# Half-row pairs for keys and values, scores in three PSUM banks, picks two batches late, first pair of row writes behind the first normalise

## The reference, cut to what matters

```python
# attention: 16 heads of 64; the last 4 of the 77 context rows have keys and values of their own
q   = xn @ Wq + lora(xn)
k,v = ctx[:73] @ Wk + lora(ctx), ctx[:73] @ Wv + lora(ctx)
out = attention(q, k, v) + attention(q, ctx[73:] @ Wk_ipa, ctx[73:] @ Wv_ipa)
x1  = x + out @ Wo + bo + lora(out)
# feed-forward: 8 experts, the best 2 of each token
logits = x2n @ gate_w                     # x2n = layernorm(x1)
top_logits, top_idx = top_k(logits, 2);   w = softmax(top_logits)
y   = x1 + sum over the two picks of w * (silu(x2n @ w1[e]) @ w2[e])
```

## Time and profile before

| what | value |
|---|---|
| median of the runs (3: 783.06, 783.86, 788.45) | 783.86 us |
| the profiled execution: its time / its span | 784.63 / 782.8 us |
| granted TensorE clock, mean of the span | 0.967 |
| busy share: PE / DVE / POOL / ACT | 87 / 68 / 63 / 58 % |
| batch bodies 1 to 14, from the first scores of one to those of the next | 27.4 us (27.7 in three of them) |

### The profile page before, as it was taken

The page is one execution under the profiler, slowest core; times in us unless marked ns, Lnnn a source line. Parts: engine busy times, 40 slices in busy tenths (PEclk is TensorE's granted clock), DMA queues, the critical chain, the costliest instruction groups (busy, mean ns, idle before and its releaser), DMA issues.

```text
span 782.8 us, 23092 instructions
## 1 busy us (share of the span) xinstructions
PE 684.6 (87%) x7980; PEld 574.2 (73%) x7981; DVE 534.7 (68%) x1226; ACT 454.8 (58%) x772; POOL 494.8 (63%) x584
## 2 busy tenths in 40 slices
PE   6747799999999999999999998751999999999994
PEld 2225688788787878878787887540888898888993
DVE  5963687877887797788779778633555565555552
ACT  1545878687776867777777777520433434344441
POOL 3125556786788678778868877853265656556565
PEclk9998899999999999999999999885999999999998
DMA  9901001111111111111111111015255555554550
GB/s 250 305 30 43 28 17 50 48 44 52 55 54 42 48 48 41 55 55 54 42 41 54 42 55 55 28 42 188 49 83 87 94 89 92 90 95 76 84 90 1
DMA packets 41676, 54.69 MB, mean 70 GB/s; under 512 B 6320, under 2 KB 36016, under 8 KB 41648
## 3 DMA queue, kind: packets, MB, share of 16 engines
q1 hardware_dynamic: 26176, 35.90, 15.7%
q0 software_dynamic: 14384, 17.33, 12.8%
q10 hardware_dynamic: 1088, 1.08, 0.4%
HBM read 30.36 MB, written 25.76 MB: 72 GB/s over the span
## 4 chain that ended last, share of the span: by engine, by line
PE 48%; DVE 16%; issue 13%; POOL 7%; ACT 6%; DMA 5%; SPq 4%; POOLq 1%; DVEq 0%; ACTq 0%
PE ps L1319 39%; DVE pt_s L1072 4%; DVE sm L1150 3%; PE ps L1380 3%; POOL prob L729 2%; PE ps L1401 2%; DVE picks L1213 2%; ACT x2n L936 2%; PE ps L439 2%; DMA pt_s<-in_wo 2%; POOL rows_dram L785 2%; DMA out_x<-pt_s,token_of 1%; POOL out_x L413 1%; DVE q_s L1072 1%; DVE x_sb L1171 1%
## 5 line engine op out<-in xcount | busy, mean ns | idle before, releaser
L413 POOL DMA_INDIRECT out_x<-pt_s,token_of x78 | 125.4, 1608 | 31.6 <-issue 30.9
L492 ACT ACTIVATE q_s<-ps 128x512 f32<-128x512 f32 x78 | 46.6, 598 | 133.1 <-PE ps L1319 132.4
L565 DVE TENSOR_TENSOR ot_s<-q_s,ot_s 128x512 f16<-128x512 f32 x78 | 54.0, 693 | 85.9 <-ACT ot_s L496 59.5
L1319 PE MATMUL ps<-q_s,ffnw 128*128 128x256 f16 x936 | 109.9, 275 | 0.0
L1319 PE MATMUL ps<-ffnw,ot_s 128*128 x936 | 108.7, 273 | 0.2 <-issue 0.2
L729 POOL TENSOR_TENSOR prob<-prob,mx 128x1168 f32<-128x1168 f32 x64 | 77.7, 1235 | 36.1 <-DVE mx L1143 35.8
L1319 PEld LDWEIGHTS ps<-ffnw,ot_s 128*128 128x128 f16 x936 | 90.2, 98 | 13.4 <-issue 2.0
L1319 PEld LDWEIGHTS ps<-q_s,ffnw 128*128 x936 | 90.6, 99 | 10.9 <-issue 0.5
L1319 PE MATMUL ps<-xt_s,wq_s 128*128 128x256 f16 x768 | 91.9, 282 | 6.4 <-DVE q_s L1072 4.5
L1319 PEld LDWEIGHTS ps<-xt_s,wq_s 128*128 128x128 f16 x768 | 77.4, 101 | 18.3 <-DVE q_s L1072 4.7
L1319 PE MATMUL ps<-wo_s,ot_s 128*128 128x256 f16 x768 | 89.2, 273 | 1.9 <-DVE ot_s L1072 1.9
(11 more groups left out here) (179 smaller groups left out, 1283.8 us busy)
## 6 DMA issues: line engine op xcount, KB each, us to landing
prob<-rows_dram SPq DMA_DIRECT2D x39, 264.0 KB
wstage<-in_ffn_w SPq DMA_DIRECT2D x16, 512.0 KB, 3.5
x_sb<-in_x SPq DMA_DIRECT2D x4, 1024.0 KB, 12.8
out_x<-x_sb SPq DMA_DIRECT2D x16, 256.0 KB, 2.2
out_x<-pt_s,token_of POOLq DMA_INDIRECT x78
rows_dram<-wstage ACTq DMA_DIRECT2D x4, 264.0 KB
rows_dram<-wstage SPq DMA_DIRECT2D x4, 264.0 KB
pt_s<-in_wq SPq DMA_DIRECT2D x2, 512.0 KB, 4.5
```

What stands on the lines that cost most here:

```text
L413: pool.indirect_dma_start(out_rows, bass.IndirectOffsetOnAxis(ap=token_of[:, j % UNROLL, c:c + 1], axis=0), y_sb[:, j % UNROLL, c, :], Non ...
L492: act.activation(h32[:, half, :], h_ps(j, half), ACT.Silu, scale=1 / WSCALE).then_inc(silu_done, 1)
L565: dve.tensor_tensor(hs[:, j % 2, 1, 2 * half:2 * half + 2, :].rearrange("p f n -> p (f n)"), h32[:, half, :], hs[:, j % 2, 0, 2 * half:2 * ...
L1319: last = pe.matmul(o, lhs(a, n), rhs(c, n), start=(i == 0), stop=(i == len(steps) - 1))
```

## The change

The diff makes five edits and rearranges the bodies around them.

1. **Half-row pairs.** The 64 rest rows of the context and of the key and value weights no longer stand above 64 zero rows. The rest rows of even head pairs (for values: of the first 512 columns) lie in partitions 0 to 63, those of odd ones in 64 to 127. A product of the rest has 64 rows, and two of them, one in each half, follow each other into two PSUM banks. The low memory fills with zeros fall away. The context rest of a batch is copied by two small transfers (ctx_k, ctx_v), issued by SP a batch ahead.
2. **Scores in three banks.** The 16 heads' scores lie 5, 5 and 6 to a bank in banks 0 to 2 (before: four in each of banks 0 to 3). A new semaphore, s_thirds, keeps the two row halves from writing one bank at a time. Other results change banks too.
3. **Late picks.** `pick_experts`, `place_rows`, `rank` and `weigh_picks` of batch b-2 run in body b; before, those of b-1 did, at the end of body b. In the last body's wake the routing of batch 14 now stands before that of 15.
4. **Row writes.** The first pair of batch b-2 stands behind `normalise(b, 0)`, the second behind `normalise(b, 1)`; before, they stood before `shift(b, 0)` and before `shift(b, 1)`.
5. **Order on PE and ACT.** Values and keys are each made in one piece; `row_high` stands between the second and third of the head results on ACT; body 1 is written out before the loop.

```diff
-        wk_s = sb("wk_s", [P, 2, KD, ID], F16)
-        wv_s = sb("wv_s", [P, 2, KD, ID], F16)
+        wk_s = sb("wk_s", [P, 2, CW], F16)
+        wv_s = sb("wv_s", [P, 2, CW], F16)
+        ctx_k = sb("ctx_k", [P, 2, ORG], F16)
+        ctx_v = sb("ctx_v", [P, 2, ORG], F16)
...
-            return ps[:, (6, 7, 4, 6)[k], :]
+            return ps[:, (6, 7, 4, 0)[k], :]
...
+        PAIR_BANKS = ((0, 1), (0, 1), (0, 1), (0, 2), (0, 2), (0, 2), (1, 2), (1, 2))
...
-            for kk, rows in enumerate((P, CDR)):
-                sp.dma_start(cstage[kk][0:rows, 0:BATCH * CTX], ctx_t[kk * P:kk * P + rows, :]
-                             ).then_inc(ctx_in[kk], 16)
+            sp.dma_start(cstage[0][:, 0:BATCH * CTX], ctx_t[0:P, :]).then_inc(ctx_in[0], 16)
+            for half in (0, 1):
+                sp.dma_start(cstage[1][half * CDR:half * CDR + CDR, 0:BATCH * CTX], ctx_t[P:CD, :]
+                             ).then_inc(ctx_in[1], 16)
...
             def body(b):
-                first, settled = isinstance(b, int) and b == 0, not (isinstance(b, int) and b < 2)
-                if settled:
-                    scatter(b - 2)
+                first, routed = isinstance(b, int) and b == 0, not (isinstance(b, int) and b < 2)
+                if routed:
+                    router_gap(b - 2)
+                    weigh_picks(b - 2)
                 shift(b, 0)
-                if settled:
-                    scatter_pick(1)
                 shift(b, 1)
                 normalise(b, 0)
+                if routed:
+                    scatter(b - 2, 0)
                 if not first:
                     rstd_2(b - 1)
                 normalise(b, 1)
+                if routed:
+                    scatter(b - 2, 1)
...
                 if not first:
-                    router_gap(b - 1)
                     row_low(b - 1)
-                    weigh_picks(b - 1)
...
                 pt(b, 6)
                 pt(b, 7)
+                ot(b, 0)
+                ot(b, 1)
                 if not first:
                     row_high(b - 1)
-                ot(b, 0)
-                if not first:
-                    gap_e(b - 1)
-                for k in range(1, 4):
-                    ot(b, k)
+                ot(b, 2)
+                ot(b, 3)
...
             def body(b, first, last):
+                routed = not (isinstance(b, int) and b < 2)
+                if routed:
+                    chain = pick_experts(b - 2)
                 maxima(b, 0)
                 if not last:
                     xt(b + 1)
+                if routed:
+                    place_rows(b - 2, chain)
                 maxima(b, 1)
...
+            def key_products(w, m, out, ctx, rest):
+
+                for half in (0, 1):
+                    o = (2 * m + half) * P
+                    for i, (a, c) in enumerate(THREE):
+                        pe.matmul(out[half], w[:, a, o:o + P], ctx(c), start=(i == 0), stop=False)
+                for i, (a, c) in enumerate(THREE):
+                    for half in (0, 1):
+                        last_of[0] = pe.matmul(
+                            out[half], w[half * CDR:half * CDR + CDR, a, ID + m * P:ID + m * P + P], rest(c, half),
+                            start=False, stop=(i == 2))
...
                 for m in range(PAIRS):
+                    if m == 6:
+                        pe.wait_ge(s_thirds, 2 * b + t + 1)
+                    if m == 3:
+                        last.then_inc(s_thirds, 1)
...
                 if not first:
                     project(b - 1, 0)
+                if not (isinstance(b, int) and b < 2):
+                    rank(b - 2)
                 scores(b, 1)
                 if not first:
                     project(b - 1, 1)
...
-                    pe.wait_ge(q_split, 4 * b + 5)
+                pe.wait_ge(s_copied, 2 * b + 2)
+                if not last:
                     queries(b + 1, 3)
-                    pe.wait_ge(q_split, 4 * b + 6)
...
+                if not last:
+                    pe.wait_ge(q_split, 4 * b + 8)
+                    pe.wait_ge(v_split, 2 * b + 1)
+                    new_keys(b + 1)
+                pe.wait_ge(v_split, 2 * b + 2)
                 transpose_probs(b, 4)
```

More of the change, by code:

```diff
@@ L976, in body @@
                 v(b, 0)
+                v(b, 1)
                 if first:
@@ L1369, in scores, with new_values @@
+            def new_values(b):
+                pe.wait_ge(ctx_v_in, 16 * b + 16)
+                value_products(wv_s, [values_bank(half)[0:ORG, :] for half in (0, 1)], lambda part: context(part, b),
+                               lambda part, half: ctx_v[half * CDR:half * CDR + CDR, part, :])
+                last_of[0].then_inc(v_mm, 1)
             def scores(b, t):
@@ L1478, in body @@
             def body(b, first, last):
-                if not first:
-                    pe.wait_ge(slots, b)
                 scores(b, 0)
@@ L1532, in body @@
                     pe.wait_ge(pt_split, 8 * b + 5 + k)
-                    if k in (1, 2) and not last:
-                        pe.wait_ge(k_split, 2 * b + 2 + k)
+                    if k == 1 and not first:
+                        pe.wait_ge(slots, b)
+                        router(b - 1)
                     attend(b, k)
-                    if k == 1 and not first:
-                        rank(b - 1)
             body(0, True, False)
-            with pe.Fori(1, BATCH - 1) as b:
+            body(1, False, False)
+            with pe.Fori(2, BATCH - 1) as b:
                 body(b, False, False)
             body(BATCH - 1, False, True)
-            for t in range(TPB):
-                project(BATCH - 1, t)
+            project(BATCH - 1, 0)
+            rank(BATCH - 2)
+            project(BATCH - 1, 1)
             transpose_2(BATCH - 1)
+            pe.wait_ge(slots, BATCH)
             router(BATCH - 1)
```

344 lines of the change are left out of this document (184 added, 160 removed).

## The result

The changed kernel takes **773.4 us** (median of 4 runs, 771.5 to 774.1), the kernel before 784.0 us in the same session: a ratio of 0.985, 95% interval 0.982 to 0.988. The forecast was 769, the range 753 to 787. The profiled execution took 773.27 us, of which 771.4 is the span.

A forecast was written before the change was run, and what follows sets the result against it. PE bound a body, POOL close behind; after the change POOL's path sets 26.45 us instead of 27.42. Bodies 2 to 15 -13.6, body 1 -2.7, body 0 -2.2, setup +0.1, tail +3.3: -15.1, so 769 us, range 753 to 787.

The forecast's parts named there:

- POOL's path: Shifts, normalises and row writes on POOL: second normalise ends at 20.25 and binds, so a body falls from 27.42 to 26.45 us.
- I take 0, since the neighbouring rows are the same kind of change: Alternating full-row and half-row products among keys and values on PE: a change of array shape costs 0.
- The late signal: ACT's first copy began 0.5 us after the scores' modelled end; taken as 0, +5 to +9 if both scores stall.
- the starts leave nothing between them: Half-row scores beside the full-row output product on PE: no gap seen in the trace, so a shape change costs 0.
- the lost 0.85 us wait: PE's gap of 0.85 us before the ranks, which waited for the picks; forecast to go.
- PE's work falls by 0.9 us: Half-row pairs in a body: keys 1.30 us instead of 1.62, values 1.98 instead of 2.58, PE's work to 24.5.
- The rival of PE's floor: POOL's path is shorter than summed, so PE binds and bodies 2 to 15 take 24.8 us: 746 us, chance 0.09.
- Body 1, body 0, setup: Body 1 without row writes, ranks or weights -2.7 us; body 0 -2.2 us; setup, with context rest rows loaded twice, +0.1.
- Tail: After the last attend, batch 14's row writes delay POOL: rstd_2 of batch 15 at 12.1 instead of 8.8, +3.3 us.
- the rival of the shape change: Shape changes lengthen the keys before the transposes of tile 1, deciding from 0.27 us each: 798 at 0.33, chance 0.09.
- PE is closed there: Sign the forecast is wrong: PE not idle before the first transposes of tile 1, where over 1 us idle was forecast.
- The second pair of writes holds ACT: Slower rival: ACT's row_high waits for the second pair's landing; at 5.0 us landing +17, 801 us, chance 0.05.

The follow-up runs named there:

- keys full: The changed kernel with the keys' last 64 context rows in full-height products against a zero-padded context tile: 764.2 us, ratio 0.974 to the kernel before.
- row_low last: The kernel before with one line moved, POOL's row_low behind the weights of the picks instead of ahead of them: 773.2 us, ratio 0.985.
- the best kernel here: "place in PSUM" with POOL's first pair of row writes between the shifts and the second behind the table's low half: 752.7 us, ratio 0.959.
- place in PSUM: "keys full" with ACT's row_high behind the last head copy and DVE's place written to PSUM instead of SBUF: 757.8 us, ratio 0.967.

## Why the prediction was right, point by point

- *The time.* 773.4 stands 4.4 us above the 769 forecast, inside its own spread of 759 to 779.
- *The bodies, right partly by luck.* 26.60 against 26.45. POOL's path was sized well: output product at 1.79 (forecast 1.75), second shift done at 11.16 (10.95), first normalise at 13.54 (13.4), guard and two writes 2.71 (3.00), `rstd_2` 1.24 (1.36), second normalise at 19.87 (20.25). But it did not bind in the changed kernel. The step that failed is "I take 0, since the neighbouring rows are the same kind of change": a change of shape costs 0.10 us, the eight at the keys 0.8, and the keys start 0.3 later than forecast (17.95). They end at 20.1, where the forecast had them at 18.95 and PE idle until 20.25. Since POOL is done at 19.87, this costs the body only the 0.08 us by which those transposes start earlier in "keys full". The second error weighs more: from the transposes of tile 1 to the end of the body I had 6.1 us, and it takes 6.49, of which 0.26 is the wait for the late signal. POOL's path, 0.38 shorter than forecast, offsets nearly all of that. With the keys repaired POOL binds at 26.19, 0.26 below the forecast.
- *The late signal, seen and put at nothing.* The forecast noted that ACT's first copy began 0.5 us after the scores' modelled end, and looked for the reason in s_thirds or the array's shape. In that trace the scores' signal is 0.49 to 1.24 us late in the 14 bodies that have row writes, where a pair begins 0.09 us before the scores' end; in "row_low last", where the pair begins 1 us behind them, it is on time in all 16. The change took the writes away from the scores and put the second pair beside the transposes of b-1.
- *The rule weighed against the trace.* The Trainium skill (TensorEngine Tiling (Array Packing), Key Properties) says that changing the tiling mode drains the TensorE. The measured 0.10 us agrees in that a change costs something, at half the latency of one key product (0.197 us) and below the 0.16 from which the forecast saw it matter. It does not look like a full drain: the next product starts 0.125 us behind the last one of the other shape, before that one's end as the profile models it. The reading "the starts leave nothing between them" was wrong. In the trace of before, too, the first full product behind the scores starts 0.125 us after the last score product, where starts within one shape are 0.03 to 0.04 apart; the merged rows hide it.
- *The source of the gain, missed in its size.* The forecast counted the lost 0.85 us wait as one of several terms on a new path. "row_low last" gets as much from that wait alone, so that the other parts of the change together come to about zero: bodies 2 to 14 0.09 us shorter (26.60 against 26.68), body 1 1.2 us shorter, setup and body 0 1.2, body 15 and the tail 3.7 longer.
- *Keys and values.* Values 2.16 against 1.98, keys 2.16 against 1.30. "PE's work falls by 0.9 us" failed: it rose by 0.1. The rival of PE's floor at 24.8 thus had no ground; the best kernel here reaches 25.57.
- *Body 1, body 0, setup.* 1.95 less against 2.7; setup and body 0 together 1.5 less against 2.1, within what the setup differs from trace to trace. *Tail*: +3.8 with body 15 against +3.3 - 1.0. `rstd_2` of batch 15 begins 11.8 us behind the last attend (forecast 12.1, before 8.8) and the expert stage 2.7 later behind it than before, so the tail was about right, and body 15 lost 1.1 instead of gaining 1.
- *Two sums.* 20.25 and 6.1 make 26.35, not the 26.45 written. In the rival of the shape change the terms given for s = 0.33, +9, +5 and +3.4, lead to 801 and not to 798. Neither changes a chance.
- *The marks.* "PE is closed there" has come true, so by its own text the forecast's mechanism is wrong in this place; keys under 2.5 us and bodies within 0.5 us of 26.4 held.
- *The second pair of writes holds ACT.* It did, but not through the landing, and ahead of its `x2t` copy instead of `row_high`: by the late signal, for 0.26 us a body on PE. No rival named that.

## What to carry to other kernels

A tiny DVE operation that takes 0.97 us beside POOL and 0.19 alone is not slow, it is held: look for its partner on POOL, and then move one of the two, or put one operand into PSUM. When an engine's chain is shortened, ask what its later work now runs beside: a pair of indirect writes that slid 2 us forward onto a TensorE signal cost more than the whole change gained. And narrow products are cheaper in half-row pairs only if the shapes change rarely; group them.

## What was unexpected in the hardware

- A DVE operation with two SBUF operands is held until POOL's running operation ends (0.97, 1.82 and 2.15 us instead of 0.18), takes its turn between two POOL operations (0.49), and is not held with one operand in PSUM (0.18). The Trainium skill (SBUF — State Buffer, "SBUF: two separate sides") describes this as an exclusive lock, for a whole instruction, on a port pair that the two engines share. These numbers agree with it; the 0.18 us beside POOL's 0.71 us operation on 2 columns, in 16 of 16 batches, does not.
- Signals of TensorE's products can come late beside POOL's indirect writes, those of ACT and DVE beside the same writes come within 0.01 us. In the kernel before, the scores' signal is 0.49 to 1.24 us late, in the changed kernel that of the transposes of b-1 1.1; for the keys it is 1.7 to 1.8 us with a pair that begins 1.1 us ahead of the product's end, 4.2 with four in a row. Away from the writes no signal of the kernel before is more than 0.11 us late. But not every signal beside them is late: the output product's, 0.9 and 2.25 us into a pair, is on time in 28 of 28 cases of the kernel before, and so is the values' 2.0 us into a pair in "place in PSUM". The transposes of b-1 end 1.6 us into the pair in the changed kernel and 1.5 in "keys full", and only the first are late. What holds the signal was not settled: no run tells the preparing of the writes from the moving of their data, and none why some signals pass.
- An idle time of 3.3 us on PE was followed by the granted clock 0.50 for the rest of the body, which made it 3.7 us longer and so doubled the price of the delay.
